# A GCN stage: epsilon added on VectorE, tiles finished four steps after their projection, carries one step ahead, and the zone's own rows scaled before the product

## What is computed

```python
edge_index = jnp.stack([src, dst])
h = jnp.maximum(_layernorm(x, axis=-1), 0.0)
x = x + _L0_gnn_ref(h, edge_index, L0_gnn_W_conv, L0_gnn_b_conv, L0_gnn_W_lin, L0_gnn_b_lin)
h = jnp.maximum(_layernorm(x, axis=-1), 0.0)        # its input for the next layer
...
# _L0_gnn_ref, with a self loop at every node
norm = deg_inv_sqrt[row] * deg_inv_sqrt[col]
h = x @ W_conv                                      # 512 -> 128
msg = h[row] * norm[:, None]
out = jax.ops.segment_sum(msg, col, num_segments=N) + b_conv
return out @ W_lin + b_lin                          # 128 -> 512
# _layernorm
return (x - m) / jnp.sqrt(v + eps)                  # m, v: mean and variance of a row
```

## Time and profile before

| | |
|---|---|
| median of three runs | 3144.35 us |
| the profiled execution, its own time | 3137.41 us |
| its span | 3135.0 us |
| PE busy | 2653.3 us (85%) |
| DVE busy | 1776.9 us (57%) |
| ACT busy | 1505.4 us (48%) |
| POOL busy | 1229.2 us (39%) |

### The profile page before, as it was taken

The page is one execution under the profiler, slowest core; times in us unless marked ns, Lnnn a source line. Parts: engine busy times, 40 slices in busy tenths (PEclk is TensorE's granted clock), DMA queues, the critical chain, the costliest instruction groups (busy, mean ns, idle before and its releaser), DMA issues. The chain is left out here.

```text
span 3135.0 us, 44137 instructions
## 1 busy us (share of the span) xinstructions
PE 2653.3 (85%) x13290; PEld 1442.5 (46%) x13290; DVE 1776.9 (57%) x3920; ACT 1505.4 (48%) x2128; POOL 1229.2 (39%) x2065
## 2 busy tenths in 40 slices
PE   0237888699989999799988969989999999899964
PEld 0225554344434444344544536655555555344443
DVE  8835776488657844798653424335555566323233
ACT  7335665355334522355335745456666666332170
POOL 3666874245322321455445511123333333101146
PEclk9998998899999999899998989999999999999976
DMA  5254442278447854666444322132222333101168
GB/s 170 84 190 123 144 146 89 96 184 203 115 114 186 203 133 109 202 217 221 148 136 121 104 75 68 57 108 101 94 97 94 104 132 131 73 1 34 42 216 310
DMA packets 366357, 405.51 MB, mean 129 GB/s; under 512 B 198251, under 2 KB 224883, under 8 KB 363516
## 3 DMA queue, kind: packets, MB, share of 16 engines
q1 hardware_dynamic: 337564, 328.83, 34.1%
q0 software_dynamic: 28640, 74.78, 8.2%
HBM read 165.00 MB, written 197.28 MB: 116 GB/s over the span
## 5 line engine op out<-in xcount | busy, mean ns | idle before, releaser
L215 PE MATMUL s_ps_z<-s_w,slots 128*128 128x512 f16 x2844 | 642.0, 383 | 41.6 <-DMA s_bias<-in_L_gnn_b 41.6
L215 PEld LDWEIGHTS s_ps_z<-s_w,slots 128*128 128x128 f16 (+1 forms) x2844 | 279.9, 99 | 360.5 <-DMA s_bias<-in_L_gnn_b 43.0
L1529 ACT ACTIVATE s_g<-s_g,s_rn 128x512 f32<-128x512 f32 x237 | 170.3, 719 | 273.1 <-POOL s_rn L1420 272.8
L1458 DVE SCALAR_TENSOR_TENSOR s_g<-s_ps_z,s_f,s_bias 128x512 f32<-128x512 f32 x237 | 177.7, 750 | 208.3 <-PE s_ps_z L215 197.1
L2198 PE MATMUL u_ps_o<-u_w,u_uT 128*128 128x512 f32 x632 | 288.6, 599 | 0.2 <-DVE u_uT L2069 0.2
L1420 POOL TENSOR_TENSOR s_rn<-s_em,minus_half 128x1 f32<-128x1 f32 x237 | 180.5, 762 | 259.9 <-DVE s_em L1473 252.0
L2180 PE MATMUL u_ps_z<-slots,u_w 128*128 (+2 forms) x1920 | 236.2, 273 | 0.0
L2306 PE MATMUL z_ps_z<-slots,z_w 128*128 128x512 f16 (+1 forms) x960 | 210.1, 378 | 7.4 <-DMA z_w<-split_root 7.4
L2180 PEld LDWEIGHTS u_ps_z<-slots,u_w 128*128 128x128 f16 x1920 | 173.6, 98 | 37.5 <-issue 0.5
L713 DVE BATCH_NORM_STATS2 u_ny_st<-u_ps_o 128x6 f32<-128x512 f32 x79 | 54.9, 694 | 212.1 <-PE u_ps_o L2198 212.1
L740 ACT ACTIVATE u_h<-u_x,u_n_sh,u_n_rs 128x512 f32<-128x512 f32 x79 | 64.3, 814 | 229.3 <-POOL u_n_sh L735 229.3
(11 more groups left out here) (367 smaller groups left out, 5488.5 us busy)
## 6 DMA issues: line engine op xcount, KB each, us to landing
h_rows<-s_g SPq DMA_DIRECT2D x158, 256.0 KB
x_rows<-q_x SPq DMA_DIRECT2D x79, 256.0 KB
s_x<-x_rows SPq DMA_DIRECT2D x79, 256.0 KB, 2.9
x_rows<-s_x SPq DMA_DIRECT2D x79, 256.0 KB, 2.1
h_rows<-s_h SPq DMA_DIRECT2D x79, 256.0 KB, 2.4
u_x<-x_rows SPq DMA_DIRECT2D x79, 256.0 KB
x_rows<-u_x SPq DMA_DIRECT2D x79, 256.0 KB
h_rows<-u_h SPq DMA_DIRECT2D x79, 256.0 KB
```

The costliest lines, as they stand in the source:

```text
L215: ins = nc.tensor.matmul(out_ap, a(c), w[:, part * size + c * n:part * size + (c + 1) * n], start=first and c == 0 and m == 0, stop=stop a ...
L1458: nc.vector.scalar_tensor_tensor(out=g[b][:, :], in0=ps_z[v.buf(4)][:, :], scalar=f[:, 0:1], in1=bias[:, :], op0=MUL, op1=ADD).then_inc(s_ ...
L1529: nc.scalar.activation(g[b][:, :], g[b][:, :], ACT.Relu, scale=rn[v.buf(2)][:, 0:1]).then_inc(s_h, 1)
```

## The change

- `PairNorm.factors` loses the instruction that adds epsilon. A new `above_eps` puts it on DVE, behind the moments of the second tile of a pair, for both norms. POOL waits for it and then computes `nm`.
- `FINISH` goes from 3 to 4; the lags written as `FINISH` + 1 and + 2 go along, and the loop gets one step more. `cT` has 4 buffers.
- `carry` moves to `FINISH - 1`, one step ahead of its tile's `convolve`, on PE and DVE, and behind the other work of that step. The gathers of edge rows stay in the steps where they were, and so do the loads of the selections.
- `diagonal` is gone. For a zone pair DVE now writes h times `dis_dst` to `hw`, which is sent to DRAM, then multiplies that by `dis_dst` once more into `hwz`; `convolve` multiplies `hwz` by the identity.

```diff
+        def above_eps(self, dve, g, n, done):
+            dve.wait_ge(self.s_mv, done)
+            nc.vector.tensor_scalar(out=self.ve[b][:, 0:n], in0=self.mv[b][:, 0:n, 1], scalar1=LN_EPS, scalar2=None,
+                                    op0=ADD).then_inc(self.s_ve, 1)
...
-            pool.wait_ge(self.s_mv, done)
-            nc.gpsimd.tensor_tensor(out=self.nm[b][:, 0:n], in0=self.mv[b][:, 0:n, 0], in1=minus_one2, op=MUL)
-            nc.gpsimd.tensor_tensor(out=self.ve[b][:, 0:n], in0=self.mv[b][:, 0:n, 1], in1=eps2, op=ADD).then_inc(
-                self.s_ve, 1)
             pool.wait_ge(self.s_ve, g + 1)
+            nc.gpsimd.tensor_tensor(out=self.nm[b][:, 0:n], in0=self.mv[b][:, 0:n, 0], in1=minus_one2[:, 0:n], op=MUL)
...
-        FINISH = 3
+        FINISH = 4
...
-            STEPS = PAIRS_ALL + ZP + 5
+            STEPS = PAIRS_ALL + ZP + FINISH + 2
...
-                    of_end(s, FINISH - 1, load_sel)
+                    of_end(s, FINISH - 2, load_sel)
...
+                        if k == len(tiles) - 1:
+                            norm.above_eps(dve, g, len(tiles), rows_done(g))
...
+                            if k == 0:
+                                wait_count(dve, hw_out[g % 2], 16 * (g // 2))
                             ins = nc.vector.tensor_scalar(
-                                out=hwz[:, e * HID:(e + 1) * HID], in0=ps_w[g % 2][:, (2 + k) * P:(3 + k) * P],
+                                out=hw[g % 2][:, k * HID:(k + 1) * HID], in0=ps_w[g % 2][:, (2 + k) * P:(3 + k) * P],
                                 scalar1=dis_dst[:, e:e + 1], scalar2=None, op0=MUL)
                         ins.then_inc(s_rows, 1)
+                        dve.wait_ge(s_rows, g + 1)
+                        for k in range(2):
+                            e = 2 * g + k
+                            nc.vector.tensor_scalar(out=hwz[:, e * HID:(e + 1) * HID], in0=hw[g % 2][:, k * HID:(k + 1) * HID],
+                                                    scalar1=dis_dst[:, e:e + 1], scalar2=None, op0=MUL).then_inc(s_hwz, 1)
...
-                    of_end(s, FINISH, lambda q: carry(q, 0))
-                    of_end(s, FINISH, lambda q: diagonal(q, 0))
-                    of_end(s, FINISH, lambda q: carry(q, 1))
...
-                    of_end(s, FINISH, lambda q: diagonal(q, 1))
                     of_end(s, FINISH, lambda q: residual(q, 0))
+                    of_end(s, FINISH - 1, lambda q: carry(q, 0))
                     of_end(s, FINISH, lambda q: residual(q, 1))
+                    of_end(s, FINISH - 1, lambda q: carry(q, 1))
...
-                        pe.wait_ge(s_diag, e + 1)
-                        nc.tensor.matmul(out_ap, hwz[:, e * HID:(e + 1) * HID], diag[e % 2][:, :], start=True, stop=False)
+                        pe.wait_ge(s_hwz, e + 1)
+                        nc.tensor.matmul(out_ap, hwz[:, e * HID:(e + 1) * HID], ident[:, :], start=True, stop=False)
...
-                    of_end(s, FINISH, lambda q: carry(q, 0))
...
                     of_end(s, FINISH, lambda q: linear(q, 1))
+                    of_end(s, FINISH - 1, lambda q: carry(q, 0))
                     of_end(s, FINISH + 1, lambda q: turn1(q, 1))
+                    of_end(s, FINISH - 1, lambda q: carry(q, 1))
```

More of the change, by code:

```diff
@@ L763, in moments, with factors @@
             nc.vector.bn_aggr(self.mv[b][:, k, :], self.stats[b][:, k, :]).then_inc(self.s_mv, 1)
-        def factors(self, pool, g, n, done, s_used, used, consts):
+        def above_eps(self, dve, g, n, done):
             b = g % 2
-            minus_one2, eps2, minus_half2 = (c[:, 0:n] for c in consts)
-            pool.wait_ge(self.s_mv, done)
-            nc.gpsimd.tensor_tensor(out=self.nm[b][:, 0:n], in0=self.mv[b][:, 0:n, 0], in1=minus_one2, op=MUL)
-            nc.gpsimd.tensor_tensor(out=self.ve[b][:, 0:n], in0=self.mv[b][:, 0:n, 1], in1=eps2, op=ADD).then_inc(
-                self.s_ve, 1)
+            dve.wait_ge(self.s_mv, done)
+            nc.vector.tensor_scalar(out=self.ve[b][:, 0:n], in0=self.mv[b][:, 0:n, 1], scalar1=LN_EPS, scalar2=None,
+                                    op0=ADD).then_inc(self.s_ve, 1)
+        def factors(self, pool, g, n, s_used, used, minus_one2, minus_half2):
+            b = g % 2
             pool.wait_ge(self.s_ve, g + 1)
+            nc.gpsimd.tensor_tensor(out=self.nm[b][:, 0:n], in0=self.mv[b][:, 0:n, 0], in1=minus_one2[:, 0:n], op=MUL)
             wait_count(pool, s_used, used)
-            nc.gpsimd.tensor_tensor(out=self.rstd[b][:, 0:n], in0=self.ve[b][:, 0:n], in1=minus_half2, op=POW).then_inc(
-                self.s_rstd, 1)
+            nc.gpsimd.tensor_tensor(out=self.rstd[b][:, 0:n], in0=self.ve[b][:, 0:n], in1=minus_half2[:, 0:n],
+                                    op=POW).then_inc(self.s_rstd, 1)
             pool.wait_ge(self.s_rstd, g + 1)
@@ L812, in gcn_layer @@
             ones3 = sb(ctx, "q_ones3", [3, P], BF16)
-            consts = [sb(ctx, f"q_{n}", [P, 2]) for n in ("minus_one", "eps", "minus_half")]
+            minus_one2, minus_half2 = sb(ctx, "q_minus_one", [P, 2]), sb(ctx, "q_minus_half", [P, 2])
             node_l = sb(ctx, "q_node_l", [P, P])
@@ L818, in gcn_layer @@
             hT = sb(ctx, "q_hT", [P, C * 2 * P])
-            cT = [sb(ctx, f"q_cT{b}", [HID, 2 * P]) for b in range(3)]
+            cT = [sb(ctx, f"q_cT{b}", [HID, 2 * P]) for b in range(4)]
             hw = [sb(ctx, f"q_hw{b}", [P, 2 * HID]) for b in range(2)]
@@ L825, in gcn_layer @@
             sl = [sb(ctx, f"q_sel{b}", [P, P]) for b in range(4)]
-            diag = [sb(ctx, f"q_diag{b}", [P, P]) for b in range(2)]
             bias_row = x1[0][0:1, :]
@@ L899, in _ @@
             def _(pool):
-                for tile, value in zip(consts, (-1.0, LN_EPS, -0.5)):
-                    nc.gpsimd.memset(tile[:, :], value).then_inc(s_const, 1)
                 nc.gpsimd.memset(ones3[:, :], 1.0).then_inc(s_const, 1)
+                nc.gpsimd.memset(minus_one2[:, :], -1.0).then_inc(s_const, 1)
+                nc.gpsimd.memset(minus_half2[:, :], -0.5).then_inc(s_const, 1)
                 nc.gpsimd.memset(beyond[:, :], float(NOWHERE)).then_inc(s_const, 1)
-                pool.wait_ge(s_const, 5)
+                pool.wait_ge(s_const, 4)
                 nc.gpsimd.affine_select(out=beyond[:, :], in_=beyond[:, :], compare_op=ALU.is_ge, fill=0.0,
@@ L1034, in carry @@
                             nc.vector.memset(m[b][0:1, :], 0.0).then_inc(s_carried, 1)
-                def diagonal(q, k):
-                    if q >= FP:
-                        e = end_pair(q)[k] - FT
-                        wait_count(dve, s_conv, e - 1)
-                        nc.vector.tensor_scalar(out=diag[e % 2][:, :], in0=ident[:, :], scalar1=dis_dst[:, e:e + 1],
-                                                scalar2=None, op0=MUL).then_inc(s_diag, 1)
                 def residual(q, k):
@@ L1053, in residual @@
                         norm1.moments(dve, x1[b][:, :], q, k, end_done(q, k))
+                        if k == len(end_pair(q)) - 1:
+                            norm1.above_eps(dve, q, k + 1, end_done(q))
                 def lo(q):
@@ L1174, in convolve @@
                         out_ap = ps_w[k][:, 0:P]
-                        if e < 4:
+                        if e < 2:
                             pe.wait_ge(s_rows, PAIRS_ALL)
```

36 lines of the change are left out of this document (15 added, 21 removed).

## The result

The changed kernel takes 3124.3 us (median of 6 runs, 3117.6 to 3126.6), the kernel before in the same company 3139.0 us (6 runs): ratio 0.9947, 95% interval 0.9932 to 0.9963. The medians are 14.7 us apart; the ratio stands for 16.6 us (11.6 to 21.3). I had forecast 13.4 us less than the profiled execution, and 3131 us from a median of 3144.35 us. The kernel before has since come out 5.3 us lower, which is most of the distance between 3131 and 3124.3. In a second measurement, r_after, the ratio was 0.9939 (0.9926 to 0.9953): 3123.1 against 3141.6 us.

What follows compares the result with a forecast made beforehand. POOL narrowly bounds steps with both passes, a DVE-PE-ACT chain the second pass's zone steps, and nobody is full in the first's. Terms: 3.4 - 9.8 + 4.6 - 2.0 - 9.6 = -13.4 us, forecast 3131 us, range 3118 to 3145.

Steps and rivals of the forecast that it cites:

- Zone pairs of the first pass: First-pass zone steps: two added DVE products, less faster epsilon, cost 0.42 us in eight steps, none in two with scatters; +3.4 us.
- POOL's instructions: Mainly steps with both passes: without epsilon on POOL a step takes 7.52 us instead of 7.91; -9.8 us in all.
- The lag of four: End of the projections: one step more, partly with the second pass alone, costs +4.6 us.
- The gap behind it: Last full pair's second residual to first zone residual: edge rows gathered one pair earlier, 15.6 us becomes 13.7; -2.0 us.
- Zone steps: Second-pass zone steps: the chain shortens from 8.07 to 7.13 us at full clock, nine times, plus 1.1 of clock; -9.6 us.
- rival 1: Second-pass zone steps: PE's clock stays up, nine steps take 64 us, -18 instead of -9.6, total 3122 us; chance 0.12.
- Rival 3: Steps with both passes: DVE's epsilon and POOL's indirect DMAs hold each other, up to 3159 us; chance 0.12.
- Rival 2: Second-pass zone steps don't shrink, staying near 9 us; -4 us in all, 3140 us, no measurable change; chance 0.20.

Runs made afterwards that it cites:

- k1_behind: The changed kernel with DVE's two products for `hwz` placed behind the pair's statistics and epsilon instead of ahead of them; ratio 0.9921 to the kernel before.
- k8_epsonly: The kernel before with only the epsilon moved from POOL to DVE, nothing else of the change; ratio 0.9983 to the kernel before.
- k2_epspool: The changed kernel with the addition of epsilon put back on POOL, behind `nm`; ratio 0.9947 to the kernel before.
- k5_finish3: The changed kernel with `FINISH` back at 3, a lag of three, nothing else; ratio 0.9933 to the kernel before.
- k6_dummy: The kernel before with eight useless PE transposes added in each zone step behind the first; ratio 0.9964 to the kernel before.
- k3_carryown: The changed kernel with the carries back in their own step, at their old places; ratio 0.9972 to the kernel before.
- k4_diag: The changed kernel with `FINISH` 3, the diagonal products back, the `hwz` products gone and three `cT` buffers; ratio 0.9947 to the kernel before.

## Why the prediction was right, and where it was not

The gain of 14.7 us lies in the forecast of 7 to 18, and the mechanism of each term is in the trace but for two: the clock in the zone steps and what the steps with scatters pay. As these two errors have opposite signs, the closeness of 13.4 and 14.7 us says little.

**Zone pairs of the first pass: mis-sized, +6.4 for +2.8** (+3.4 for the products less 0.6 for POOL). The step that failed is "Eight steps pay; in the two others POOL's scatters are the bound and cover it". Six of the eight grew by 0.45, from 5.45 to 5.90, close to the 0.42 of the prediction. In the two steps with scatters POOL's gather waits for DVE's statistics, which the products delay: 6.45 and 6.51 before became 7.30 and 7.47, +1.8 where -0.6 was booked. The fourth and the eighth step grew by 0.9 and 1.1 instead of 0.45, to 6.35 and 6.51, at a granted clock of 0.92 and 0.89; in r_after the eighth is 5.90 at 1.00. But the second step took 5.90 at 0.71, so the clock by itself doesn't explain them, and no run does. k1_behind has the products behind the statistics, and its steps with scatters are 6.11 and 6.27, its ten pairs 55.5 us; k8_epsonly, without the products, has 55.4. So the order was the price, not the work.

**POOL's instructions: the mechanism right, the size 2 us too large.** 7.51 for 7.52; k2_epspool and k8_epsonly isolate it (6.1 and 7.7 us over the 29 steps). What is missing lies in the last ten of these steps. I had counted a gain of some 3 us there, and they took 76.8 after 75.3, two of them 9.9 and 9.6 at a granted clock of 0.90 and 0.74. Part of it is epsilon: a step in which PE works without a pause at full clock is 6.97 us with epsilon on DVE (the change, k5_finish3) and 6.75 with it on POOL (before, k2_epspool). The rest comes and goes with the clock: the same ten steps took 75.1 us in k5_finish3 and 78.9 in k2_epspool.

**The lag of four: +7.3 in place of +6.0 for its late part.** From the last rows to the last full pair's second residual there were 3.35 us and are 10.66. I had 6.0 for the step with the second pass alone, taken from steps at full clock; the granted clock fell to half within it (0.76 on average), and it was 7.6. The gap behind it was right (-1.9). By the prediction the lag cost 4.6 - 2.0 = 2.6 us in net; by k5_finish3 it costs about 6.

**Zone steps: -21.2 in place of -9.6, and this is rival 1.** The failed step is "What the lowered clock costs, 82.2 - 9 x 8.07 = 9.6 us, shrinks with the time: 1.1". It shrank to nothing in the first profile, and to 1.6 in r_after, whose first zone step took 8.22 us. The chain itself gave 9 x (8.07 - 6.77) = 11.7 against the 8.5 predicted, the clock 9.5 against 1.1. k6_dummy shows the clock's share by itself: the chain of before with a busier PE loses 10.0 us of the 82.2. PE was busy 60.5 of 82.2 us before, in part at the lower clock, and 50.0 of 61 after. The Trainium skill says in "TensorE: Matmul & The Clock Gate", section "HAM oscillation", that pauses between bursts bring the slow clock back; k6_dummy agrees, in that filling the pauses of PE took the granted clock from 0.86 to 1.00. k3_carryown and k4_diag show that it takes only one of the two edits undone for the clock to fall again in some steps: 0.50 us more of chain cost 1.1 us a step in k3_carryown (against the first profile), 0.90 cost 1.8 in k4_diag.

**Rival 3, DVE and POOL holding each other, did not come at its size.** The epsilon in the window of the earlier trace rows, and over the whole stage:

```profile
L768 DVE TENSOR_SCALAR q_norm_ve<-q_norm_mv x23: 168/170/217, 343.5 to 426.0; 128x2 f32<-128x2 f32 x23
L768 DVE TENSOR_SCALAR q_norm_ve<-q_norm_mv x80: 153/170/399, 203.9 to 590.3; 128x2 f32<-128x2 f32 x78, 128x1 f32<-128x1 f32 x2
```

In the window it is 0.217 us at most, beside a POOL that is busy 70 of 87 us, and steps of 7.51, as worked out, leave no room for a late start on the loop. In the stage one of 80 took 0.40, at 460.55 beside an indirect DMA of POOL, and again at 460.25 in r_after: a quarter of a microsecond once, where the rival needed a mean hold of 0.7 to turn the kernel slower. The Trainium skill speaks in "SBUF — State Buffer", section "Who interferes with whom", of a block for as long as the other holds the ports; this trace shows no block of that length with this instruction, and no run here shows whether it uses the shared ports at all. Rival 2 is out with the zone steps of 6.77.

## What to carry to other kernels

An instruction that nobody waits for soon goes behind the last one that somebody does wait for: the same two products, in ten steps, cost 7 us ahead of the statistics and nothing behind them. Where a chain leaves TensorE waiting, count the clock with it, since shortening the chain a little can give back as much again, and so can useless work. Before adding up savings found one by one, ask of each which wait it hides behind: the lag of three saved 6 us of the changed kernel's stage, and cost 26 us (358.4 to 384.4) once the carries stood ahead of the residuals.
